# Per-sequence row transfers on the queues of SyncE and ScalarE in a routed three-class MLP with layer norm

## The chip, the cores and the metric

One core of one Trainium2 chip runs the kernel. The metric is the device time of one execution in microseconds (us). Engines are named as in the profile: PE is TensorE, DVE VectorE, ACT ScalarE, POOL GpSimd, SP SyncE; SPq and ACTq are the DMA issues of two of them.

## What is computed

There are 64 sequences of 64 tokens with 256 features. Each sequence has a class from 0 to 2, and only the class's own branch counts:

```python
out_nr  = gelu(x @ w1_nr  + b1_nr)  @ w2_nr  + b2_nr          # class 0
out_tsr = gelu(x @ w1_tsr + b1_tsr) @ w2_tsr + b2_tsr         # class 1
h = gelu(x @ w1_sr + b1_sr)                                   # class 2, 512 wide
out_sr = gelu(h @ w2_sr + b2_sr) @ w3_sr + b3_sr
y = x + where(class == 0, out_nr, where(class == 1, out_tsr, out_sr))
return (y - mean(y)) * rsqrt(var(y) + 1e-5) * gamma + beta
```

The classes are data, known only on the chip. In these inputs they are 23, 26 and 15 sequences.

## The kernel before

**Groups.** The kernel sorts the sequences by class and packs them, 8 at a time, into groups of one class. There are 11 slots for groups (`SLOTS`), at least 8 of them are used (`MIN_GROUPS`), and with these inputs 9 are: 2 of class 2 (called SR, "long"), 4 of class 1 (TSR) and 3 of class 0 (NR), the last 7 being "short". Group g lives in the buffer `xs[g]`, 128 partitions by 4 tokens by 256 features; a sequence is 16 partitions of it, a row 4 KB. With 9 groups there are 72 places and 64 sequences, so 8 places stay empty.

**Table.** DVE and PE compute where each sequence goes (L500 to L541): each sequence's rank within its class, the group in which its class begins (`base`, L523), then `passed`, `nth`, `in_place`, `in_slot` and `row_at` (L521 to L531), a PE product of the last two (L705) and from it the index tables `load_idx` (L538) and `store_idx` (L540). `cls_tab` (L548) holds the class of each group, and every engine loads it into registers and branches on it.

**Rows in and out.** POOL fetches a group with one indirect DMA (`gather`, L299), three of them as soon as `load_idx` is there (`EARLY = 3`) and eight after its weight work (L316). It stores a group with one indirect DMA (`scatter`, L354). SP issues the weights, waits for the first group (L253) before it issues those of the other two classes, and at the end waits for all stores.

**Work of a step.** In step s, PE transposes the rows of group s+1 (L713), makes layer 1 of group s (L732 to L734; `short_first` or `long_first`) and the last layer of group s-1 (`last_layer`, L777 to L788), and for a long group the middle layer (L806 to L808). Each product is three matmuls, since operands are split in a high and a low part. Before its first transposes PE runs ten warm-up matmuls (L814). ACT makes the high parts and the gelus, DVE the low parts, `y` and its moments (L568 to L598; the last of these is `hvar`, which releases POOL). The norm of a group goes over three engines: POOL's power `rstd` (`root`, L331) and `shift` (L335), ACT's z in four tiles (L413), POOL's times gamma (L341) and plus beta (L346) for tiles 0 to 2, DVE's (L603, L605) for tile 3.

**Order on POOL.** `middle(g)` (L359) is root(g), shifted(g), times_gamma(g-1), plus_beta(g-1), scatter(g-1). `final(g)` (L367), for the last group, is times_gamma(g-1) on two tiles, root(g), plus_beta(g-1), scatter(g-1), scatter(g); DVE then takes two tiles of group g-1 (`gamma_beta_two`) and all of group g (L625, L631). `by_place` (L213) chooses between these by the classes of the next groups; PE's `to_f` and `to_x` are the same `last_layer` into `ps_f` or, for the last group, into `ps_x`.

## Time and profile before

| | us |
|---|---|
| median of 3 runs | 112.78 (111.09 to 112.89) |
| the profiled execution | 111.2 |
| its span, first to last instruction | 109.5 |
| PE busy in it | 86.0 |
| POOL busy in it | 68.3 |

The profiled execution took 111.2 us, of which the span is 109.5 us, so 1.7 us lie around the span. The profile gives starts and durations in us from the span's start. "Idle before" and its releaser are inferred from semaphore events; "issue" is time for which the profile shows nothing awaited. Instructions that issue DMAs, load registers or branch are not counted as busy.

### The profile page before, as it was taken

What the parts mean: (1) busy time and instruction counts of PE and PEld (TensorE: products, weight loads), DVE (VectorE), ACT (ScalarE), POOL (GpSimd) and SP (SyncE); (2) the same over time, 40 slices, a digit from 0 to 9 for tenths busy, and PEclk for the clock granted to TensorE, in tenths of its full rate; (3) what the DMA queues carried; (4) which work ended last, traced back from release to release, by engine and by line L of the source; (5) the groups of instructions that cost most, each with busy time, mean ns of one, the idle gap of its engine ahead of it and who ended that gap; (6) DMA issues with size and microseconds to landing.
All of it is one profiled execution on the core that took longest, in us unless ns stands there. A gap on an engine that the chain in (4) does not pass through costs nothing.

```text
span 109.5 us, 1829 instructions
## 1 busy us (share of the span) xinstructions
PE 86.0 (79%) x503; PEld 74.9 (68%) x503; DVE 77.6 (71%) x193; ACT 64.3 (59%) x104; POOL 68.3 (62%) x78
## 2 busy tenths in 40 slices
PE   0269969999999999999999999999999976600000
PEld 0157568868889888798998989989899866500000
DVE  5579084762555572839989899899998889699800
ACT  0575229995986045895977959779595870330000
POOL 6427910019777630000796988979879798999850
PEclk9999999999999999999999999999999999995555
DMA  0794788100498991000000404022040130103153
GB/s 2 264 311 142 234 258 298 34 0 3 94 343 205 419 407 73 0 6 0 0 6 22 175 3 174 6 87 105 6 192 6 73 130 6 54 0 154 40 216 144
DMA packets 5459, 12.84 MB, mean 117 GB/s; under 512 B 688, under 2 KB 2752, under 8 KB 5440
## 3 DMA queue, kind: packets, MB, share of 16 engines
q0 software_dynamic: 2880, 9.96, 25.5%
q1 hardware_dynamic: 2540, 2.63, 7.3%
q8 instruction: 11, 0.18, 0.7%
q14 instruction: 8, 0.07, 0.2%
q10 hardware_dynamic: 20, 0.01, 0.0%
HBM read 8.40 MB, written 4.72 MB: 120 GB/s over the span
## 4 chain that ended last, share of the span: by engine, by line
PE 67%; POOL 13%; DVE 4%; DMA 4%; issue 4%; POOLq 2%; ACT 1%; ACTq 1%
PE ps_a L732 8%; PE ps_a L734 8%; PE ps_a L733 7%; PE ps_x L713 7%; PE ps_f L786 6%; PE ps_f L788 6%; PE ps_f L787 6%; POOL xs L346 4%; POOL xs L341 4%; PE ps_f L814 4%; DMA bias_rows<-L_cond_b_sr_dram 4%; PE ps_f L777 3%; POOL rstd L331 3%; PE ps_b L807 2%; PE ps_b L808 2%
## 5 line engine op out<-in xcount | busy, mean ns | idle before, releaser
L331 POOL TENSOR_TENSOR rstd<-hvar,half 128x4 f32<-128x4 f32 x9 | 9.4, 1040 | 15.6 <-DVE hvar L598 15.5
L788 PE MATMUL ps_f<-wf_hi,f_hi 128*128 x64 | 17.9, 280 | 0.0
L786 PE MATMUL ps_f<-wf_hi,f_lo 128*128 x64 | 17.9, 280 | 0.0
L787 PE MATMUL ps_f<-wf_lo,f_hi 128*128 x64 | 17.9, 280 | 0.0
L732 PE MATMUL ps_a<-x_hi,w_lo 128*128 128x512 f32 x40 | 16.5, 413 | 1.1 <-DVE x_lo L643 1.1
L409 ACT ACTIVATE f_hi<-ps_a,bias_cols 128x512 fp32r<-128x512 f32 x16 | 11.0, 688 | 9.6 <-PE ps_a L808 4.7
L734 PE MATMUL ps_a<-x_hi,w_hi 128*128 128x512 f32 x40 | 15.7, 393 | 0.0
L733 PE MATMUL ps_a<-x_lo,w_hi 128*128 128x512 f32 x40 | 15.6, 390 | 0.0
L299 POOL DMA_INDIRECT xs<-x_dram,load_idx x11 | 11.1, 1012 | 6.5 <-DVE load_idx L538 3.6
L413 ACT ACTIVATE xs<-xs,shift,rstd 128x256 f32<-128x256 f32 x23 | 12.1, 593 | 4.3 <-POOL shift L335 4.3
L346 POOL TENSOR_TENSOR xs<-xs,beta_b 128x768 f32<-128x768 f32 (+1 forms) x8 | 14.1, 1762 | 0.5
L410 ACT ACTIVATE ps_a<-ps_a,bias_cols 128x512 f32<-128x512 f32 x22 | 14.4, 652 | 0.0
L341 POOL TENSOR_TENSOR xs<-xs,gamma_b 128x768 f32<-128x768 f32 (+1 forms) x8 | 14.2, 1779 | 0.0
L564 DVE TENSOR_TENSOR f_lo<-ps_a,f_hi 128x512 fp32r<-128x512 f32 x16 | 10.5, 685 | 3.5 <-ACT ps_a L410 3.1
L568 DVE TENSOR_TENSOR xs<-ps_f,xs 128x1024 f32<-128x1024 f32 x8 | 9.8, 1225 | 4.2 <-PE ps_f L788 4.2
L787 PEld LDWEIGHTS ps_f<-wf_lo,f_hi 128*128 128x128 f32 x64 | 12.0, 188 | 0.7
L786 PEld LDWEIGHTS ps_f<-wf_hi,f_lo 128*128 128x128 f32 x64 | 12.1, 188 | 0.3
L788 PEld LDWEIGHTS ps_f<-wf_hi,f_hi 128*128 128x128 f32 x64 | 12.1, 190 | 0.0
L572 DVE BATCH_NORM_STATS2 stats<-xs 128x6 f32<-128x256 f32 x32 | 11.3, 414 | 0.3
L354 POOL DMA_INDIRECT out_dram<-xs,store_idx x9 | 9.4, 1043 | 3.2 <-POOL xs L346 2.0
L405 ACT ACTIVATE x_hi<-ps_x 128x1024 fp32r<-128x1024 f32 x8 | 8.2, 1027 | 4.0 <-PE ps_x L713 4.0
L313 POOL TENSOR_TENSOR wf_lo<-wf_raw,wf_hi 128x512 fp32r<-128x512 f32 x3 | 4.0, 1337 | 10.2 <-ACT wf_hi L395 10.2
(124 smaller groups left out, 191.3 us busy)
## 6 DMA issues: line engine op xcount, KB each, us to landing
w_raw<-L_cond_w_sr_dram SPq DMA_DIRECT2D x2, 512.0 KB, 4.6
wf_raw<-L_cond_w_sr_dram SPq DMA_DIRECT2D x1, 256.0 KB, 5.3
w_raw<-L_cond_w_tsr_dram SPq DMA_DIRECT2D x1, 256.0 KB, 6.5
w_raw<-L_cond_w_nr_dram SPq DMA_DIRECT2D x1, 256.0 KB, 6.8
wf_raw<-L_cond_w_tsr_dram SPq DMA_DIRECT2D x1, 256.0 KB, 6.9
wf_raw<-L_cond_w_nr_dram SPq DMA_DIRECT2D x1, 256.0 KB, 7.1
xs<-x_dram,load_idx POOLq DMA_INDIRECT x11, 6.5
out_dram<-xs,store_idx POOLq DMA_INDIRECT x9, 3.4
```

Source lines behind the costliest of these rows:

```text
L331: nc.gpsimd.tensor_tensor(rstd[:, g, :], hvar[:, g, :], half[:, :], ALU.pow).then_inc(rstd_step, 1)
L341: nc.gpsimd.tensor_tensor(tiles, tiles, spread(gamma_b, n), ALU.mult).then_inc(gam_pool, 1)
L346: nc.gpsimd.tensor_tensor(tiles, tiles, spread(beta_b, n), ALU.add).then_inc(o_pool, 1)
L410: nc.scalar.activation(bank, bank, ACT.Gelu, bias=bias).then_inc(gelu_done, count)
L413: nc.scalar.activation(dst, xs[g][:, t, :], ACT.Identity, bias=shift[:, g, t:t + 1], scale=rstd[:, g, t:t + 1]).then_inc(z_done, 1)
L572: nc.vector.bn_stats(stats[:, t, :], xs[g][:, t, :]).then_inc(bn_done, 1)
L732: nc.tensor.matmul(dst, w1_lo[:, kt, cols], xh[:, kt, :], start=(kt == 0), stop=False)
L733: nc.tensor.matmul(dst, w1_hi[:, kt, cols], xl[:, kt, :], start=False, stop=False)
L734: mm = nc.tensor.matmul(dst, w1_hi[:, kt, cols], xh[:, kt, :], start=False, stop=(kt == KT - 1))
L786: nc.tensor.matmul(dst, fl[:, kt, toks], w_hi, start=False, stop=False)
L787: nc.tensor.matmul(dst, fh[:, kt, toks], w_lo, start=False, stop=False)
L788: mm = nc.tensor.matmul(dst, fh[:, kt, toks], w_hi, start=False, stop=last)
```

## The change

The index tables go. A table `place_tab` of 2 rows of 88 places holds the number of the sequence at each place and a 1 where there is one. SP and ACT load its entries into registers and issue one plain DMA of 64 KB (16 partitions) for each sequence: SP for all groups but the second half of group 0, which ACT fetches, and the second half of the last group, which ACT stores. All 88 places of the 11 slots are fetched; a store of an empty place is issued with a condition that skips it. `EARLY` is 2: SP issues its half of group 0 and all of group 1, then the weights of the other classes, then the other nine slots, then the stores in order. POOL issues no DMA, runs times gamma ahead of the power, and takes three tiles of the last group but one. `each_step` replaces `by_place`: each step is written out whole for the long class and for the short ones, with the variant for "no further group" (`finish`) ahead of it.

```diff
+        def load_places(eng, regs, row, s, first, n, hi):
+            eng.load(regs[0:n], place_tab[0:1, row, s * PER + first:s * PER + first + n])
+            return [eng.snap(r, min_val=0, max_val=hi) for r in regs[0:n]]
+
+        def x_of(seq):
+            return x[bass.ds(seq, 1), :, :].rearrange("a (q t) h -> (a q) t h", t=TT)
+
+        def out_of(seq):
+            return out[bass.ds(seq, 1), :, :].rearrange("a (q t) h -> (a q) t h", t=TT)
+
+        def rows_of(s, j):
+            return xs[s][j * ROWS:(j + 1) * ROWS, :, :]
+
+        def each_step(eng, cls, step, finish):
+
+
+            for s in range(SLOTS + 1):
+                if s < MIN_GROUPS:
+                    step(s)
+                elif s < SLOTS:
+                    with eng.If(cls[s] > NR):
+                        if s == MIN_GROUPS:
+                            finish(s - 1)
+                        else:
+                            with eng.If(cls[s - 1] < EMPTY):
+                                finish(s - 1)
+                            with eng.Else():
+                                pass
                     with eng.Else():
-                        last(g)
+                        step(s)
                 else:
+                    with eng.If(cls[s - 1] < EMPTY):
+                        finish(s - 1)
+                    with eng.Else():
+                        pass
...
+        def if_next(eng, cls, s, part):
+
+            if s + 1 < MIN_GROUPS:
+                part(s + 1)
+            elif s + 1 < SLOTS:
+                with eng.If(cls[s + 1] < EMPTY):
+                    part(s + 1)
...
-
-            sp.wait_ge(x_loaded[0], 16)
+            seq_regs = [sp.alloc_register(f"sp_seq{j}") for j in range(PER)]
+            taken_regs = [sp.alloc_register(f"sp_taken{j}") for j in range(PER)]
+
+            def fetch(s, n):
+                seqs = load_places(sp, seq_regs, 0, s, 0, n, B - 1)
+                for j in range(n):
+                    sp.dma_start(rows_of(s, j), x_of(seqs[j])).then_inc(x_loaded[s], 16)
+
+
+            sp.wait_ge(place_tab_done, 1)
+            fetch(0, PER // 2)
+            for s in range(1, EARLY):
+                fetch(s, PER)
             for i in (2, 3):
                 sp.dma_start(W_L1[i][0], W_L1[i][1]).then_inc(w_in[i], 16)
             for i in (1, 2):
                 sp.dma_start(W_F[i][0], W_F[i][1]).then_inc(w_in[4 + i], 16)
+            for s in range(EARLY, SLOTS):
+                fetch(s, PER)
             sp.wait_ge(tab_done, 1)
             cls = load_classes(sp, "sp_cls")
-            for s in range(SLOTS):
+
+            def store(g, n):
+                taken = load_places(sp, taken_regs, 1, g, 0, n, 1)
+                seqs = load_places(sp, seq_regs, 0, g, 0, n, B - 1)
+                if n == PER:
+                    sp.wait_ge(o_pool, g + 1)
+                sp.wait_ge(o_dve, 2 * (g + 1))
+                for j in range(n):
+                    sp.dma_start(out_of(seqs[j]), rows_of(g, j), cond=(taken[j] > 0)).then_inc(stored[g], 16)
+
+            def sp_step(s):
+                if s > 0:
+                    store(s - 1, PER)
+            each_step(sp, cls, sp_step, lambda g: store(g, PER // 2))
+            for s in range(MIN_GROUPS - 1):
+                sp.wait_ge(stored[s], 16 * PER)
+            for s in reversed(range(MIN_GROUPS, SLOTS)):
                 with sp.If(cls[s] < EMPTY):
-                    sp.wait_ge(stored[s], 16)
+                    sp.wait_ge(stored[s], 16 * PER)
                 with sp.Else():
                     pass
+            sp.wait_ge(stored[MIN_GROUPS - 1], 16 * PER)
...
-            def gather(s):
-                nc.gpsimd.indirect_dma_start(
-                    out=xs[s][:, :, :].rearrange("p t h -> p (t h)"), out_offset=None, in_=x_rows,
-                    in_offset=bass.IndirectOffsetOnAxis(ap=load_idx[:, s:s + 1], axis=0)
-                ).then_inc(x_loaded[s], 16)
-
-            pool.wait_ge(load_idx_done, 1)
-            for s in range(EARLY):
-                gather(s)
-
...
-            for s in range(EARLY, SLOTS):
-                gather(s)
...
-            def scatter(g, last):
-                if g == 0:
-                    pool.wait_ge(store_idx_done, 1)
-                if not last:
-                    pool.wait_ge(o_pool, g + 1)
-                pool.wait_ge(o_dve, 2 * (g + 1))
-                nc.gpsimd.indirect_dma_start(
-                    out=out_rows, out_offset=bass.IndirectOffsetOnAxis(ap=store_idx[:, g:g + 1], axis=0),
-                    in_=xs[g][:, :, :].rearrange("p t h -> p (t h)"), in_offset=None,
-                    bounds_check=last_row, oob_is_err=False).then_inc(stored[g], 16)
-
+            def pool_group(g):
+                if g > 0:
+                    times_gamma(g - 1, POOL_TT)
                 root(g)
                 shifted(g)
                 if g > 0:
-                    times_gamma(g - 1, POOL_TT)
                     plus_beta(g - 1, POOL_TT)
-                    scatter(g - 1, False)
-
-            def final(g):
-                times_gamma(g - 1, 2)
+
+            def pool_step_of(s):
+                if s > 0:
+                    pool_group(s - 1)
+
+            def pool_finish(g):
+                times_gamma(g - 1, POOL_TT)
                 root(g)
-                plus_beta(g - 1, 2)
-                scatter(g - 1, False)
-                scatter(g, True)
-
-            for g in range(SLOTS):
-                with pool.If(cls[g] < EMPTY):
-                    by_place(pool, cls, g, middle, middle, final)
-                with pool.Else():
-                    pass
+                plus_beta(g - 1, POOL_TT)
+
+            each_step(pool, cls, pool_step_of, pool_finish)
...
+            seq_regs = [act.alloc_register(f"act_seq{j}") for j in range(PER // 2)]
+            taken_regs = [act.alloc_register(f"act_taken{j}") for j in range(PER // 2)]
             w_high(0)
+            act.wait_ge(place_tab_done, 1)
+            for j, seq in enumerate(load_places(act, seq_regs, 0, 0, PER // 2, PER // 2, B - 1)):
+                act.dma_start(rows_of(0, PER // 2 + j), x_of(seq)).then_inc(x_loaded[0], 16)
             w_high(1)
             wf_high(0)
             act.wait_ge(bf_in, 16 * 3)
...
+            def act_finish(g):
+                normed(g - 1)
+                n = PER // 2
+                taken = load_places(act, taken_regs, 1, g, n, n, 1)
+                seqs = load_places(act, seq_regs, 0, g, n, n, B - 1)
+                act.wait_ge(o_dve, 2 * (g + 1))
+                for j in range(n):
+                    act.dma_start(out_of(seqs[j]), rows_of(g, n + j), cond=(taken[j] > 0)).then_inc(stored[g], 16)
+
+            each_step(act, cls, act_step, act_finish)
...
-            dve.wait_ge(dve_step, step[0] - 1)
-            nc.vector.tensor_scalar(passed[:, :], full[:, :], rank[:, 0:1], None, ALU.is_le).then_inc(dve_step, 1)
             dve.wait_ge(dve_step, step[0])
-            nc.vector.tensor_reduce(base[:, :], over_before[:, :, :], AX.XY, ALU.add).then_inc(dve_step, 1)
-            step[0] += 2
-            dve.wait_ge(dve_step, step[0] - 1)
-            chain(nc.vector.tensor_reduce(nth[:, :], passed[:, :], AX.X, ALU.add))
-            chain(nc.vector.scalar_tensor_tensor(out=in_place[:, :], in0=nth[:, :], scalar=-float(PER),
-                                                 in1=rank[:, :], op0=ALU.mult, op1=ALU.add))
-            nc.vector.tensor_scalar(in_slot[:, :], slot_id[:, :], base[:, 0:1], nth[:, 0:1],
-                                    ALU.subtract, ALU.is_equal).then_inc(place_done, 1)
-            nc.vector.scalar_tensor_tensor(out=row_at[:, :], in0=row_place[:, :], scalar=in_place[:, 0:1],
-                                           in1=row_val[:, :], op0=ALU.is_equal, op1=ALU.mult
-                                           ).then_inc(place_done, 1)
+            chain(nc.vector.tensor_reduce(base[:, :], over_before[:, :, :], AX.XY, ALU.add))
+            chain(nc.vector.scalar_tensor_tensor(out=place[:, :], in0=base[:, :], scalar=float(PER), in1=rank[:, :],
+                                                 op0=ALU.mult, op1=ALU.add))
+            nc.vector.tensor_scalar(at_place[:, :], place_id[:, :], place[:, 0:1], None, ALU.is_equal
+                                    ).then_inc(at_place_done, 1)
 
             chain(nc.vector.tensor_reduce(groups[:, :], over[0:1, :, :], AX.X, ALU.add))
             chain(nc.vector.tensor_tensor_scan(ends[:, :], groups[:, :], zeros[:, :], 0.0, ALU.add, ALU.add))
-            dve.wait_ge(rows_ps, 1)
-            nc.vector.tensor_scalar(load_idx[:, :], rows_pt, float(NROWS), float(NROWS - 1), ALU.add, ALU.min
-                                    ).then_inc(load_idx_done, 1)
-            nc.vector.tensor_scalar(store_idx[:, :], rows_pt, float(NROWS), None, ALU.add
-                                    ).then_inc(store_idx_done, 1)
+            dve.wait_ge(places_ps, 1)
+            nc.vector.tensor_copy(place_tab[:, :, :], places_pt).then_inc(place_tab_done, 1)
             for r in range(ROUTES):
                 nc.vector.tensor_scalar(ended[:, :, r], slot_id[0:1, :], ends[:, r:r + 1], None, ALU.is_ge
...
-                dve.wait_ge(z_done, TT * g + (1 if n == 1 else TT))
-                nc.vector.tensor_tensor(tiles, tiles, spread(gamma_b, n), ALU.mult).then_inc(gam_dve, 1)
+            def gamma_beta_one(g):
+                dve.wait_ge(z_done, TT * g + 1)
+                nc.vector.tensor_tensor(ps_z[:, 0, 0:H], ps_z[:, 0, 0:H], gamma_b[:, :], ALU.mult).then_inc(gam_dve, 1)
                 dve.wait_ge(gam_dve, g + 1)
-                nc.vector.tensor_tensor(out_tiles, tiles, spread(beta_b, n), ALU.add).then_inc(o_dve, 2)
-
-            def gamma_beta_one(g):
-                gamma_beta(g, ps_z[:, :, 0:H], xs[g][:, TT - 1:TT, :], 1)
-
-            def gamma_beta_two(g):
-                gamma_beta(g, ps_a[0][:, 0, :].rearrange("p (t h) -> p t h", t=2), xs[g][:, 2:TT, :], 2)
+                nc.vector.tensor_tensor(xs[g][:, TT - 1, :], ps_z[:, 0, 0:H], beta_b[:, :], ALU.add
+                                        ).then_inc(o_dve, 2)
...
-            pe.wait_ge(place_done, 2)
-            nc.tensor.matmul(rows_pt, row_at[:, :], in_slot[:, :], start=True, stop=True).then_inc(rows_ps, 1)
+            pe.wait_ge(at_place_done, 1)
+            nc.tensor.matmul(places_pt[:, 0, :], seq_ones[:, 0:1], at_place[:, :], start=True, stop=True)
+            nc.tensor.matmul(places_pt[:, 1, :], seq_ones[:, 1:2], at_place[:, :], start=True, stop=True
+                             ).then_inc(places_ps, 1)
...
-                pe.wait_ge(x_loaded[g], 16)
+                pe.wait_ge(x_loaded[g], 16 * PER)
...
+            def pe_step(s):
                 if s > 0:
-                    with pe.If(cls[s - 1] < EMPTY):
-                        by_place(pe, cls, s - 1, to_f, to_f, to_x)
+                    pe.wait_ge(x_lo_done, upto_x(s))
+                    if_next(pe, cls, s, transpose_x)
+                with pe.If(cls[s] < TSR):
+                    long_first(s)
+                    if s > 0:
+                        last_layer(s - 1, ps_f)
+                    long_second(s)
+                with pe.Else():
+                    with pe.If(cls[s] < NR):
+                        short_first(TSR, s)
                     with pe.Else():
-                        pass
-                if s < SLOTS:
-                    with pe.If(cls[s] < TSR):
-                        long_second(s)
+                        short_first(NR, s)
+                    if s > 0:
+                        last_layer(s - 1, ps_f)
+
+            each_step(pe, cls, pe_step, lambda g: last_layer(g, ps_x))
```

The same recasting into `act_step`, `dve_step_of` and `pool_step_of` keeps the order of ACT's and DVE's instructions within a step; DVE takes one tile of the last group but one where it took two, and POOL three where it took two.

On POOL, the end of the program as it runs with 9 groups; before, the group before the last and the last. The names are those of the lines above, with `xs7` the last group but one.

```order
L331 TENSOR_TENSOR rstd<-hvar,half 128x4
L335 TENSOR_TENSOR shift<-rstd,neg_mean 128x4
L341 TENSOR_TENSOR xs6<-xs6,gamma_b 128x768
L346 TENSOR_TENSOR xs6<-xs6,beta_b 128x768
L354 DMA out_dram<-xs6,store_idx 1024x1024
...
L341 TENSOR_TENSOR xs7<-xs7,gamma_b 128x512
L331 TENSOR_TENSOR rstd<-hvar,half 128x4
L346 TENSOR_TENSOR xs7<-xs7,beta_b 128x512
L354 DMA out_dram<-xs7,store_idx 1024x1024
L354 DMA out_dram<-xs8,store_idx 1024x1024
```

And now:

```order
L370 TENSOR_TENSOR xs6<-xs6,gamma_b 128x768
L360 TENSOR_TENSOR rstd<-hvar,half 128x4
L364 TENSOR_TENSOR shift<-rstd,neg_mean 128x4
L375 TENSOR_TENSOR xs6<-xs6,beta_b 128x768
...
L370 TENSOR_TENSOR xs7<-xs7,gamma_b 128x768
L360 TENSOR_TENSOR rstd<-hvar,half 128x4
L375 TENSOR_TENSOR xs7<-xs7,beta_b 128x768
```

Gamma stands ahead of the power, the three DMAs are gone, and the last two products have 768 columns for 512.

On SP, the store of the last group, as it runs with 9 groups; before, SP's rows there are only branches and waits. An ISA row computes an address from a register, TENSOR_LOAD fills the registers (once for the sequence numbers, once for the ones that say a place is taken).

```order
L209 TENSOR_LOAD place_tab
L210 ISA
L209 TENSOR_LOAD place_tab
L210 ISA
L296 ISA
L296 DMA out_dram<-xs8 16x1024
L296 ISA
L296 DMA out_dram<-xs8 16x1024
L296 ISA
L296 DMA out_dram<-xs8 16x1024
L296 ISA
L296 DMA out_dram<-xs8 16x1024
```

The store of any other group has eight such DMAs on SP, and in the fetch there is one address row for each DMA too.

## Rows read from the trace of the kernel before

**Rows 1.** The page, part 4: the chain that ended last, by engine.

```profile
PE 67%; POOL 13%; DVE 4%; DMA 4%; issue 4%; POOLq 2%; ACT 1%; ACTq 1%
```

**Rows 2.** Busy time by stretch, with TensorE clock, DMA share and GB/s.

```profile
core 0: us, PE busy (x) PEld busy (x) DVE busy (x) ACT busy (x) POOL busy (x), PEclk, DMA share, GB/s
42.20:83.40 41.20, 41.20 (x276) 37.54 (x275) 35.06 (x84) 33.83 (x56) 26.91 (x24) 1.00 0.14 53
105.00:106.00 1.00, 0.00 (x0) 0.00 (x0) 0.00 (x0) 0.00 (x0) 0.83 (x1) 0.50 0.89 360
```

**Rows 3.** Timeline of the start: start us, us, instruction [idle before <-releaser].

```profile
5.29 0.17 DVE L523 TENSOR_REDUCE base<-over_before 64x1 f32<-64x32 f32 x1
...
5.99 0.34 DVE L531 SCALAR_TENSOR_TENSOR row_at<-row_place,in_place,row_val 64x128 f32<-64x128 f32 x1
...
7.09 0.17 DVE L538 TENSOR_SCALAR load_idx<-ps_b 128x11 int32<-128x11 f32 x1 [0.49 <-PE ps_b L705]
7.13 1.06 ACT L391 ACTIVATE w_hi<-w_raw 128x1024 fp32r<-128x1024 f32 x1 [0.45 <-DMA w_raw<-L_cond_w_sr_dram]
...
7.35 4.64 PE L814 MATMUL ps_f<-warm_x,ones 128*128 128x512 f32 x10
...
11.91 1.30 PEld L713 LDWEIGHTS ps_x<-ident,xs 128*128 128x128 f32 x8 [0.65 <-DMA xs<-x_dram,load_idx]
...
14.48 0.19 PEld L732 LDWEIGHTS ps_a<-x_hi,w_lo 128*128 128x128 f32 x1 [1.27 <-issue]
...
15.97 1.03 PE L713 MATMUL ps_x<-ident,xs 128*128 128x128 f32 x8
```

**Rows 4.** DMA issues: the timeline of SPq, and the page, part 6 (us to landing).

```profile
4.32 0.24 SPq L247 DMA_DIRECT2D bf_raw<-L_cond_b_tsr_dram  x1
4.61 0.25 SPq L247 DMA_DIRECT2D bf_raw<-L_cond_b_nr_dram  x1
4.90 0.36 SPq L250 DMA_DIRECT2D gamma_b<-L_cond_gamma_dram  x1
...
cond_col<-itok_B_dram SPq DMA_DIRECT2D x1, 0.2 KB, 2.3
out_dram<-xs,store_idx POOLq DMA_INDIRECT x9, 3.4
```

**Rows 5.** Timeline of POOL at the end.

```profile
93.39 1.05 POOL L331 TENSOR_TENSOR rstd<-hvar,half 128x4 f32<-128x4 f32 x1
...
94.67 1.81 POOL L341 TENSOR_TENSOR xs<-xs,gamma_b 128x768 f32<-128x768 f32 x1
...
99.72 1.28 POOL L341 TENSOR_TENSOR xs<-xs,gamma_b 128x512 f32<-128x512 f32 x1
...
101.97 1.26 POOL L346 TENSOR_TENSOR xs<-xs,beta_b 128x512 f32<-128x512 f32 x1
103.51 1.05 POOL L354 DMA_INDIRECT out_dram<-xs,store_idx  x1 [0.29 <-POOL xs L346]
104.87 0.96 POOL L354 DMA_INDIRECT out_dram<-xs,store_idx  x1 [0.30 <-issue]
```

**Rows 6.** Timeline of DVE and ACT at the end.

```profile
92.83 0.16 DVE L598 SCALAR_TENSOR_TENSOR hvar<-m,diff 128x4 f32<-128x4 f32 x1
...
93.71 0.42 DVE L605 TENSOR_TENSOR xs<-ps_z,beta_b 128x256 f32<-128x256 f32 x1
...
94.96 0.70 DVE L579 TENSOR_TENSOR ps_x<-ps_x,xs 128x512 f32<-128x512 f32 x1 [0.83 <-PE ps_x L788]
95.75 1.04 ACT L413 ACTIVATE ps_a<-xs,shift,rstd 128x256 f32<-128x256 f32 x2
...
98.64 0.19 DVE L598 SCALAR_TENSOR_TENSOR hvar<-m,diff 128x4 f32<-128x4 f32 x1
...
102.02 1.66 DVE L631 SCALAR_TENSOR_TENSOR xs<-ps_x,rstd,beta_b 128x256 f32<-128x256 f32 x4
```

**Rows 7.** Timeline of PE where the last group's last layer begins.

```profile
91.19 0.49 PE L777 MATMUL ps_x<-bf_parts,ones 128*128 x1 [1.54 <-issue]
```

More of the change, by code:

```diff
@@ L80, in build_cond_mlp @@
         rank = sb("rank", [B, 1])
-        full = sb("full", [B, PER])
-        passed = sb("passed", [B, PER])
-        nth = sb("nth", [B, 1])
-        in_place = sb("in_place", [B, 1])
         slot_id = sb("slot_id", [B, SLOTS])
-        in_slot = sb("in_slot", [B, SLOTS])
-        row_place = sb("row_place", [B, P])
-        row_val = sb("row_val", [B, P])
-        row_at = sb("row_at", [B, P])
-        load_idx = sb("load_idx", [P, SLOTS], I32)
-        store_idx = sb("store_idx", [P, SLOTS], I32)
+        place_id = sb("place_id", [B, PLACES])
+        seq_ones = sb("seq_ones", [B, 2])
+        place = sb("place", [B, 1])
+        at_place = sb("at_place", [B, PLACES])
+        place_tab = sb("place_tab", [1, 2, PLACES], I32)
         groups = sb("groups", [1, ROUTES])
```

226 lines of the change are left out of this document (73 added, 153 removed).

## The prediction

> **What bounds the kernel now.** I read first the chain that ended last, then busy time by stretch, then the timelines of the two ends. The chain gives PE 67% and POOL 13% [rows 1]. The stretches say where each rules: from 42.2 to 83.4 us PE is busy for all of the 41.2 us, while POOL is busy for 26.91 [rows 2]. There, taking POOL's DMA work away or giving SP more to do is worth nothing, provided rows arrive in time. So the change can act at two places: the start, and the end behind PE, where POOL's ordered list (power, gamma, beta, store) and then the last stores set the end.
>
> At the start ten warm-up matmuls run from 7.35 to 11.99, and the first transposes follow at once; the rows of group 0 were there at 11.91, when PE's loads stopped waiting for that DMA [rows 3]. Two things end together: earlier rows alone gain nothing. At the end POOL's last product ends at 101.97 + 1.26 = 103.23, the last scatter is issued at 104.87 [rows 5], lands about 3.4 us later [rows 4] at 108.3, and some 1.2 us on the span ends at 109.5.
>
> **The table chain.** Before, it went from `base` (5.29) over `in_place` and `row_at` (5.99 + 0.34) and PE to `load_idx`, done at 7.26 [rows 3]. Now it is `base`, `place`, `at_place`, PE, one copy: three instructions fewer ahead of PE, about 0.5 us, so the table stands at 6.8. POOL's two memsets of weight parts move up beside this chain and may give part of that back.
>
> **The fetches.** SP must load registers. The trace shows no such load alone; after its first transposes PE loads 11 registers in an idle stretch of at most 1.27 us [rows 3], so 0.5 us for four is my estimate, and 0 to 1.3 the bound. Then comes the cost on which everything hangs: the interval between two plain 64 KB DMAs on one queue, with an address row for each. Call it d. From below: two tiny DMAs on SP start 0.29 us apart [rows 4]. From above: POOL's two last indirect issues start 1.36 us apart [rows 5]. One over 128 partitions occupied SP for 0.36 us [rows 4]. Sixteen partitions lie between the tiny and the wide one, and the address row adds something; I take d = 0.37. For the landing after an issue, the tiniest took 2.3 and a scatter 3.4 us [rows 4]; I take 2.6.
>
> SP's four and ACT's four of group 0 start at 7.3 to 8.4 and land at 11.0, 0.9 us before the warm-ups end. SP's eight of group 1 begin after another load at 9.4, the last at 12.0, landing at 14.6; PE transposes them at 15.97 [rows 3], a margin of 1.4 us. The four issues on ACT stand ahead of its weight copy that began at 7.13 [rows 3] and push that and two small copies back by 2 us; ACT's next job is the high part of x after the transposes that start at 11.91, so this is covered with about 1.5 us to spare. The later weights go out at about 12.4 instead of when group 0 landed, near 11.9: half a microsecond on loads that are read ten microseconds later. The other 72 fetches take 72 x 0.37 = 27 us of SP beside PE's work; each group has a step of nearly 7 us, so it pays until d is above 0.8. Start: 0.
>
> **POOL at the end.** PE no longer idles 1.54 us before the last layer of the last group [rows 7], if that idle time came from the long way in the code to it: `finish` now follows at once. DVE waited 0.83 us for PE there [rows 6], so its sums start when its previous product ends, 93.71 + 0.42 = 94.1, and the last `hvar`, done at 98.83, is done at 98.0. POOL waited for no one at 93.39 but its own scatter; `hvar` of group 7 was ready at 92.99 [rows 6]. So power and shift end at 93.0 + 1.35 = 94.35. ACT's four z took to 96.79 from 94.7 [rows 5, 6], so now until 96.45. Then POOL: gamma on three tiles 1.81 [rows 5] to 98.3, power 1.05 to 99.35, beta on three tiles, 1.8 by the same row, to 101.15. Before this end was 103.23: 2.1 us earlier. Split: two scatters between groups out, the third tile (some 0.5 us for each product) in. Gamma ahead of the power hides gamma in the wait for `hvar`; its price is that the last power starts 0.3 us after its `hvar`. DVE's four last products (1.66 us, [rows 6]) are ready at about 102.5, before SP reaches them.
>
> **The stores at the end.** Here the change pays back. Group 7 is eight DMAs on SP, ready at 101.15, and four of group 8 follow on the same queue; ACT's other four run beside them. SP's last starts 11 intervals on: 101.25 + 11 x 0.37 = 105.3. Landing 2.6, then the same 1.2 us: 109.1. The stores thus start 2.1 us sooner, their issue takes 4.0 us where two scatters needed 1.6 from 103.23, and the landing is 0.8 shorter. The waits that SP now walks at its end lie under that landing.
>
> **Sum.** 109.1 against 109.5: -0.4 us. The profiled execution would be 110.8 for 111.2; that execution lies 1.6 us under the median of the runs, 112.78, and on that scale I say 112.4. The forecast's own range: d = 0.29 and landing 2.3 give 101.25 + 3.2 + 2.3 + 1.2 = 107.9, d = 0.45 and landing 3.4 give 110.8, so 111.2 to 114.1. About 2% (2.3 us) is what a measurement of this kernel can tell from no change.
>
> **Rival 1, narrow transfers (slower).** Each DMA now covers 16 of 128 partitions. If such a transfer cannot use the whole width, its rate falls. The whole width moved 360 GB/s in the stores' stretch [rows 2]; one part in eight of the partitions could be held to anything between an eighth and all of that. At a quarter, 90 GB/s, 64 KB take 0.73 us, and both queues share it. End: 15 real stores, 101.25 + 14 x 0.73 + 2.6 + 1.2 = 115.3. Start: group 0 lands at 7.3 + 7 x 0.73 + 2.6 = 15.0, 3.0 us late, and group 1 adds up to 2. Together 9 to 11 us. If transfers overlap in part, an effective 0.5 us gives 112 at the end and half a microsecond at the start: 112.8, or 116 on the scale of the median. I price this rival at 117. It decides from an interval of 0.42, where the end is what it was. For it: nothing in the profile shows narrow large transfers keeping their rate. Against it: successive sequences touch different partitions and could overlap. The middle would hide it either way.
> The Trainium skill speaks against the change here: "SBUF — State Buffer", section "Door 1: The DMA port swizzle", says that bandwidth follows the SBUF ports reached and gives 104 GB/s for partitions 0 to 15; 64 KB would take 0.63 us. By it, as an estimate, the end is at 113.9 and the start 3 us late. No row here shows it.
>
> **Rival 2, PE's way through the code.** The long and short variants are now written out whole, so at step 8 PE skips more. In the instruction lists, before, PE skipped 104 rows between the last layer of step 7 and the first product of step 8 without a gap, and 183 rows before the 1.54 us of [rows 7]. Now it skips about 131 at step 8 and none at step 9. If 131 is already too many, the idle time moves to 83.4, where DVE and POOL follow PE closely, and group 7's `hvar` and all behind it come 1.4 us later: 110.5, or 113.8 on the scale of the median.
> The Trainium skill, "Runtime: NRT & Kernel Launch", section "Instruction fetch mechanics", says that a taken branch to a target outside the two pages held stalls for a fetch. The gap in the trace agrees with such a rule, but does not show its cause.
>
> **Rival 3, faster.** If the issue is as cheap as the tiny DMAs', landing is 2.0 and the closing time shrinks with POOL's queue empty, the span is 107.2: 110.3 on the scale of the median. For it: POOL's end improves by 2.1 in any case. Against it: twelve issues in a row on one queue.
>
> **How the numbers follow.** Forecast 45%, rival 1 30%, rival 2 10%, rival 3 15%. Beyond 2% faster: rival 3 and a little of the forecast's edge, 0.18. Slower: rival 1 less its mild part, and the edge of the forecast with rival 2's, 0.33. The rest, 0.49, is within 2%. The range runs from rival 3 to just above the priced rival 1: 110.2 to 118.5.
>
> **What would show it.** In the new trace: DMA issues on SP at intervals near 0.37 (0.6 and more: rival 1, or a dear issue); transposes of group 0 at 11.9 and of group 1 near 16.0 without a wait for the DMA; POOL's last product ending near 101.2; no PE gap at 83.4 and none before the last layer; SP's last store starting near 105.3. The forecast is wrong if the landing of group 7's stores grows with each of them, or if PE waits for rows at any step.

## The result, and the profile after

The changed kernel takes 130.44 us (median of 4 runs, 130.06 to 130.92) where the kernel before takes 112.03 (111.09 to 112.89): a ratio of 1.173, interval 1.168 to 1.179. Two of the four executions of the kernel before (112.78 and 112.89) fell in a slower state of the chip, so the ratio is against the other two, 111.09 and 111.28, and the 1.6 us that the forecast added for "the scale of the median" come from that state. The forecast was 112.4, with a range up to 118.5. It was wrong, far outside the range.

The profiled execution took 130.06 us, its span is 128.2 us (before 109.5). The page of the changed kernel, its parts 1 to 4 in extract (PEclk is the granted TensorE clock in tenths):

```profile
PE 89.4 (70%) x505; PEld 76.7 (60%) x505; DVE 77.7 (61%) x189; ACT 64.5 (50%) x104; POOL 48.5 (38%) x58
...
PE   0296399999999999999999999999996000000000
...
PEclk9999855999999999999999999999999755555555
DMA  1958485342343432533314525262443422562633
...
q1 hardware_dynamic: 7180, 12.14, 40.7%
...
PE 61%; DVE 12%; DMA 5%; issue 2%; ACTq 2%; ACT 1%; DVEq 1%
```

No engine is busier than before by more than 0.2 us, apart from PE's 3 us, and POOL has lost the 20 us that were to go. Yet in the last nine slices of 40, some 28 us, PE does nothing, while the DMA engines go on, two to six tenths busy. The chain of waits [as rows 1] ends in products of DVE at 108.3 and shows little of what follows, since DMA issues are no busy time. What follows is in the timeline of SP's queue (start us, us from the start of the first issue to the end of the last, instruction, count), the answer to [rows 4]:

```profile
8.24 6.83 SPq L273 DMA_DIRECT2D xs<-x_dram  x12
...
18.04 46.07 SPq L273 DMA_DIRECT2D xs<-x_dram  x72
67.31 58.72 SPq L296 DMA_DIRECT2D out_dram<-xs  x68
```

These last two rows are the whole result. SP fetches until 64.1, reads its tables for 3.2 us, and then stores without a pause until 126.0; 2.2 us later the span ends. Group 0 was ready at 60.49, when POOL's last product on it ended; its stores begin at 67.3, 6.8 us late. From group to group the stores are 7.06 us apart on average (5.6 to 8.8), while groups come every 6.99 and the last two sooner, so the backlog never goes away: group 7 is ready at 107.04 and its first store starts at 117.6. Computation ended long before; timelines of POOL and DVE, the answer to [rows 5, 6]:

```profile
58.63 1.86 POOL L375 TENSOR_TENSOR xs<-xs,beta_b 128x768 f32<-128x768 f32 x1
...
102.07 1.68 DVE L589 TENSOR_TENSOR diff<-stats 128x4 f32<-128x4 f32 x1
...
106.65 1.65 DVE L627 SCALAR_TENSOR_TENSOR xs<-ps_x,rstd,beta_b 128x256 f32<-128x256 f32 x4
...
104.25 1.02 POOL L360 TENSOR_TENSOR rstd<-hvar,half 128x4 f32<-128x4 f32 x1 [0.52 <-DVE hvar L599]
105.24 1.80 POOL L375 TENSOR_TENSOR xs<-xs,beta_b 128x768 f32<-128x768 f32 x1
```

The first row is POOL's last product on group 0. POOL is done at 107.04, DVE at 108.3. The start is worse too; the timeline of PE, ACT's queue and SP's, the answer to [rows 3]:

```profile
8.20 2.00 ACTq L445 DMA_DIRECT2D xs<-x_dram  x4
...
13.88 1.10 PE L698 MATMUL ps_x<-ident,xs 128*128 128x128 f32 x8 [2.05 <-DMA xs<-x_dram]
...
16.18 0.77 PE L713 MATMUL ps_a<-x_hi,w_lo 128*128 128x512 f32 x1 [1.21 <-DVE x_lo L639]
```

PE waits 2.05 us for the first rows, 13.88 instead of 11.91. With that idle time behind it its granted clock falls from 2.4 to 1.2 GHz (the two 5s in PEclk): products follow each other at 0.43 us instead of 0.23 from 16.2 to 22.4. The next steps are 4.8 us late: the transposes of step 2 start at 46.80 for 42.01.

What one issue costs is in the instructions of the fetch's line, the store's line and the register load's, on SP (count: duration in ns, least/median/most):

```profile
L273 SPq MOVE xs<-x_dram x84: 29/29/38, 8.2 to 63.7; - x84
L273 SPq DMA_DIRECT2D xs<-x_dram x84: 315/316/1407, 8.2 to 63.8; - x84
L273 SPq FUSED_REGOPS  x73: 37/37/43, 8.6 to 63.7; - x73
...
L296 SPq FUSED_REGOPS  x68: 174/174/200, 67.0 to 125.4; - x68
L296 SPq DMA_DIRECT2D out_dram<-xs x68: 73/315/1170, 67.3 to 125.7; - x68
...
L209 SPq TENSOR_LOAD <-place_tab x29: 298/524/545, 7.4 to 123.1; - x29
```

A fetch mostly starts 0.50 us after the one before, a store 0.63, since the register step (FUSED_REGOPS) takes 174 ns with the condition and 37 without. A store that its condition skips still takes 0.40. A group of eight adds its register loads: across one load two fetches start 1.26 us apart, and between the last store of a group and the first of the next lie 2.2, with two loads. Now and then an issue takes up to 1.4 us; the trace shows no cause. With all this a group of fetches takes 5.12 us on average (46.07 / 9) and one of stores 7.06.

### The profile page after: what moved, and what is told of

It is laid out like the page before. It is cut to its first block, busy times and chain, and to the rows that moved or that the text cites. A ratio compares the mean times of both kernels' runs of the same rounds, so it can differ in the third digit from the quotient of the medians.

```text
span 128.2 us, 2202 instructions
## 1 busy us (share of the span) xinstructions
PE 89.4 (70%) x505; PEld 76.7 (60%) x505; DVE 77.7 (61%) x189; ACT 64.5 (50%) x104; POOL 48.5 (38%) x58
## 4 chain that ended last, share of the span: by engine, by line
PE 61%; DVE 12%; DMA 5%; issue 2%; ACTq 2%; ACT 1%; DVEq 1%
PE ps_a L713 8%; PE ps_a L714 8%; PE ps_a L715 8%; PE ps_x L698 7%; PE ps_f L766 6%; PE ps_f L767 6%; PE ps_f L765 6%; DMA xs<-x_dram 3%; PE ps_f L756 3%; DMA cond_col<-itok_B_dram 2%; PE ps_b L780 1%; PE ps_b L779 1%; PE ps_b L781 1%; DVE diff L589 1%; DVE ps_x L621 1%
## 5 line engine op out<-in xcount | busy, mean ns | idle before, releaser
L370 POOL TENSOR_TENSOR xs<-xs,gamma_b 128x768 f32<-128x768 f32 x8 | 14.7, 1838 | 12.0 <-ACT xs L429 12.0
L713 PE MATMUL ps_a<-x_hi,w_lo 128*128 128x512 f32 x40 | 17.7, 443 | 1.2 <-DVE x_lo L639 1.2
L714 PE MATMUL ps_a<-x_lo,w_hi 128*128 128x512 f32 x40 | 16.5, 414 | 0.0
L715 PE MATMUL ps_a<-x_hi,w_hi 128*128 128x512 f32 x40 | 16.5, 412 | 0.0
L375 POOL TENSOR_TENSOR xs<-xs,beta_b 128x768 f32<-128x768 f32 x8 | 14.8, 1846 | 0.0
L429 ACT ACTIVATE xs<-xs,shift,rstd 128x256 f32<-128x256 f32 x24 | 12.6, 592 | 0.0
L698 PE MATMUL ps_x<-ident,xs 128*128 128x128 f32 x72 | 10.3, 290 | 2.0 <-DMA xs<-x_dram 2.0
L698 PEld LDWEIGHTS ps_x<-ident,xs 128*128 128x128 f32 x72 | 8.9, 150 | 3.3 <-DMA xs<-x_dram 2.8
```

Of the source, the lines that this page charges most:

```text
L370: nc.gpsimd.tensor_tensor(tiles, tiles, spread(gamma_b, n), ALU.mult).then_inc(gam_pool, 1)
L375: nc.gpsimd.tensor_tensor(tiles, tiles, spread(beta_b, n), ALU.add).then_inc(o_pool, 1)
L429: nc.scalar.activation(dst, xs[g][:, t, :], ACT.Identity, bias=shift[:, g, t:t + 1], scale=rstd[:, g, t:t + 1]).then_inc(z_done, 1)
L698: mm = nc.tensor.transpose(ps_x[:, kt, t * P:(t + 1) * P], xs[g][:, t, kt * P:(kt + 1) * P], ident[:, :])
L713: nc.tensor.matmul(dst, w1_lo[:, kt, cols], xh[:, kt, :], start=(kt == 0), stop=False)
L714: nc.tensor.matmul(dst, w1_hi[:, kt, cols], xl[:, kt, :], start=False, stop=False)
```

## The experiments

e1, e2, e3, e4, e7, e8 and e10 are one execution each. The spans of the changed kernel's four executions go from 128.2 to 129.2 us, so a difference of 1 us in them says nothing.

**e1, fewer fetches.** Two of the eleven slots hold nothing for this input; the change fetches rows for them all the same. Here SP skips them.

```diff
-            for s in range(EARLY, SLOTS):
+            for s in range(EARLY, MIN_GROUPS):
                 fetch(s, PER)
...
+            for s in range(MIN_GROUPS, SLOTS):
+                with sp.If(cls[s] < EMPTY):
+                    fetch(s, PER)
```

> SP does not fetch the two slots that stay empty (16 of 88 fetches). Theory A (SP's stream of issues is the bound: about 5.1 us per slot fetched, 7.1 us per group stored, back to back from 67.3 us): the stores begin when group 0 is ready, near 60.6, not 67.3, and the span falls by those 6.7 us to 121.5; the other 3.5 us of the saving turn into waiting for group 0. Theory B (narrow transfers move their bytes slowly): about the same fall, so this run tells A and B from a third, that the end is set by compute: then nothing changes, 128.

Measured: 120.42 us, span 118.6, 2.9 us below the expectation. With sixteen issues fewer on SP the span is 9.6 us shorter. SP's rows:

```profile
18.16 37.38 SPq L273 DMA_DIRECT2D xs<-x_dram  x56
59.05 57.24 SPq L301 DMA_DIRECT2D out_dram<-xs  x68
```

The stores start 8.3 us sooner, and the end follows. Not all of it is the edit's. SP is free at 55.5 and now waits for group 0, which is ready at 58.71: the fetches held the stores up by the 6.8 us of the changed kernel. Group 0 is ready 1.8 us sooner here, as PE's lower clock lasted 3.4 us and not 6.8 in this execution, and the stores took 1.5 us less. So the rows that nobody reads cost about 7 us, over a third of the loss.

**e2, the same count, fewer bytes.** The sixteen fetches stay, with 8 KB each instead of 64.

```diff
+                    if s < 9:
                         sp.dma_start(rows_of(s, j), x_of(seqs[j])).then_inc(x_loaded[s], 16)
+                    else:
+                        sp.dma_start(rows_of(s, j)[:, 0:1, 0:128], x_of(seqs[j])[:, 0:1, 0:128]).then_inc(x_loaded[s], 16)
```

> The 16 fetches of the empty slots are still issued, but carry 8 KB each, not 64 KB. Theory A (cost per issued DMA): SP's interval stays 0.50 us, the first store still starts near 67.3, span 128. Theory B (cost per byte in a transfer of 16 partitions): SP gets through these 16 some 6 us sooner, first store near 61, span 121.5.

Measured: 128.79 us, span 127.0.

```profile
17.98 35.85 SPq L274 DMA_DIRECT2D xs<-x_dram  x56
54.77 8.95 SPq L276 DMA_DIRECT2D xs<-x_dram  x16
66.93 57.85 SPq L299 DMA_DIRECT2D out_dram<-xs  x68
```

With an eighth of the bytes the sixteen still take 8.95 us of SP (9.34 in the changed kernel), and the stores start at 66.93 for 67.31. The span is 1.2 us shorter, hardly more than two executions differ. From 64 KB down to 8 KB the price is by the DMA, not by the byte.

**e3, e4, e5: one side at a time.** Three kernels keep the change's layout of the code and its order on POOL (gamma ahead of the power) and give back POOL's indirect DMAs for the stores (e3), for the fetches (e4) and for both (e5). The long table chain is back too; e3 and e4 make both tables, which starts PE 0.5 us later (first transposes at 14.40 for 13.88, and 12.52 for e5's 12.00). The core of the edits, as POOL has it again:

```diff
+            def gather(s):
+                nc.gpsimd.indirect_dma_start(
+                    out=xs[s][:, :, :].rearrange("p t h -> p (t h)"), out_offset=None, in_=x_rows,
+                    in_offset=bass.IndirectOffsetOnAxis(ap=load_idx[:, s:s + 1], axis=0)
+                ).then_inc(x_loaded[s], 16)
...
-            def store(g, n):
...
+                    scatter(g - 1, False)
```

> Fetches stay one plain DMA per sequence on SP, stores go back to one indirect DMA per group on POOL (with the old index tables beside the new one). Theory A with a late start: rows of group 0 come 2 us late and the TensorE clock falls once, 4.7 us as in the changed kernel, plus about 0.3 for the longer table chain; the end is POOL's: span 113 to 114. If the stores' backlog is not the main cost: above 120.

> Fetches go back to indirect DMAs on POOL, stores stay per sequence on SP. Theory A: no late start (transposes at 12.0, full clock); SP stores from about 56 us at 7.1 us per group, a little slower than groups get ready, so it is 3 to 4 us behind at the last two, and then eight and four more issues: span 116 to 118. If the rows' late start mattered more than the stores: below 113.

> Everything of the change but its DMAs: fetches and stores are indirect on POOL as before, with gamma ahead of the power, three tiles on POOL for the last group but one, and the steps written out. If the DMAs per sequence are the whole loss: span 108.3 to 109.5 and a ratio of 0.98 to 1.00 to the kernel before. If the new code layout costs PE time at its jumps: a gap on PE near 83 us and 110 or more.

Measured, as spans, so that the rows can be compared: before 109.5; e5 112.0; e3 116.2; e4 117.0; the change 128.2. From e5, fetches by SP cost 4.2 us, stores by SP 5.0, both 16.2: 7.0 us more than the two together. That surplus is the shared queue, where the stores of group 0 wait 6.8 us for the fetches. In e4, with SP free for stores, its rows read

```profile
57.38 57.45 SPq L301 DMA_DIRECT2D out_dram<-xs  x68
```

It begins as soon as group 0 is ready and keeps pace with PE (6.8 us a group, where groups come every 6.96), but after POOL's last product at 103.39 it still has twelve stores and two sets of register loads to issue: the last starts at 114.5. The times are 118.03 us (e3, span 2.2 above its expectation, which left out what e5 loses) and 118.7 (e4, as expected). e5 has four executions: 113.68 us, ratio 1.021 (1.017 to 1.025), span 2.5 above before. The expectation was a gain, and it missed; e6 and e9 look for the cause.

**e6, gamma ahead of the power alone.** The kernel before with this one edit:

```diff
+                if g > 0:
+                    times_gamma(g - 1, POOL_TT)
                 root(g)
                 shifted(g)
                 if g > 0:
-                    times_gamma(g - 1, POOL_TT)
```

> The kernel before with one change: on POOL, times gamma of the group before runs ahead of the power and shift. Theory: POOL's list at the end shortens, since gamma of groups 5 and 6 runs in POOL's waits for DVE: span 107.6, 1.9 less, ratio 0.983. Rival: root is held up by ACT's z and nothing is gained: 109.5.

Measured: 112.24 us, ratio 1.009 (1.0065 to 1.0116). A small loss, clear of its interval, instead of a gain. DVE and POOL in e6:

```profile
92.81 1.11 DVE L589 TENSOR_TENSOR diff<-stats 128x4 f32<-128x4 f32 x1
...
92.03 1.85 POOL L341 TENSOR_TENSOR xs<-xs,gamma_b 128x768 f32<-128x768 f32 x1
```

`diff` is an operation on 128x4 that takes 0.17 us elsewhere. Here it ends at 93.92, when POOL's gamma ends, 93.88. The last `diff` takes 0.93 in the same way, behind gamma at 98.87. So gamma, meant to fill POOL's wait for `hvar`, holds up the very chain on DVE that makes `hvar`: group 7's is ready at 94.34 where it was 92.99. The Trainium skill, "SBUF — State Buffer", section "SBUF: two separate sides", says that VectorE and GpSimd share a port pair that one of them can lock; the rows agree with that rule.

**e7, a warm start.** Fifteen warm-up matmuls instead of ten, so that PE is idle for less time ahead of the rows.

> The changed kernel with 15 warm-up matmuls, not 10, so that PE works until about 13.8 us, when the rows of group 0 land. Theory (the idle 2 us let the granted clock fall to half from 16 to 22 us, which costs 2.9 us): the clock stays full, the end of compute moves from 108.3 to 105.4. The span stays near 128, because SP's issues set it. Rival (the clock falls whatever PE does ahead): compute ends at 108.3 or later.

Measured: 131.62 us, span 129.9. PE is idle for 1.39 us instead of 2.05, the clock stays at its full level, and steps come 2.85 us sooner (43.95 for 46.80). The end does not: SP's stores start at 68.09 and take 59.56. The lower clock costs 2.9 us of computation and, in this kernel, nothing of the time. The span is even 1.7 us longer, by longer pauses between SP's issues, whose cause is not known.

**e8, no registers for the fetch.** Sequence numbers fixed when the kernel is built; no register load, no address step. The kernel leaves out the sorting by class at the fetch, so sequences pass through another class's branch; the work is the same.

```diff
-                seqs = load_places(sp, seq_regs, 0, s, 0, n, B - 1)
                 for j in range(n):
-                    sp.dma_start(rows_of(s, j), x_of(seqs[j])).then_inc(x_loaded[s], 16)
+                    sp.dma_start(rows_of(s, j), x_of((s * PER + j) % B)).then_inc(x_loaded[s], 16)
```

> SP's fetches take their sequence number from the place number at build time: no register load and no address row in a fetch (so the rows of the sequences are mixed up). Theory: the interval of two fetches falls from 0.50 to about 0.36 us, a slot from 5.1 to about 3.5 us, the stores begin near 60 when group 0 is ready, span 121.5. If the interval stays at 0.50, the DMA itself and not the address work sets it.

Measured: 123.27 us, span 121.4, as expected, though the interval of two fetches fell to 0.46 and not to 0.36. The 72 fetches take 37.35 us instead of 46.07 and end at 52.4; the stores start at 61.03, as soon as group 0 is ready (60.7). But the first transposes come later still, at 14.56. The fetch's instructions from 16 to 24 us, and after them part 2 of the page, 3 us to a slice:

```profile
L272 SPq DMA_DIRECT2D xs<-x_dram x18: 419/420/429, 16.0 to 23.9; - x18
...
DMA to landing us min/median/max: 5.0/5.1/5.2
```

```profile
DMA  2879999999995444430036261644426231266533
GB/s 22 316 221 178 131 271 222 149 144 144 151 161 127 132 112 119 104 92 0 0 65 108 38 100 35 103 76 80 85 49 103 51 54 23 50 108 105 95 65 68
```

These fetches land 5.1 us after their issue; in the changed kernel it is 2.1 (median of all). From 21 to 36 us the DMA engines are taken up by nine tenths or more and move 144 to 161 GB/s. The stores of before moved 360 at 0.89 [rows 2]. Transfers of 16 neighbouring partitions are thus held to some 150 GB/s here, 0.44 us for 64 KB: just under the issue interval. The queue shows the same: the landing grows from 2.1 to 4.8 us over SP's first eight fetches, which share the DMA engines with ACT's four, then falls by some 0.01 us from one fetch to the next, and is back at 2.2 from 38 us on. There the DMA engines are busy for 0.46 of the time, and the interval is 0.46 us still: the issue sets it, and not the transfer.

**e9, the layout of the code alone.** e5 with POOL's order as before: what is left is PE's, DVE's and ACT's new code and the third tile for POOL in group 7.

```diff
-                if g > 0:
-                    times_gamma(g - 1, POOL_TT)
                 root(g)
                 shifted(g)
                 if g > 0:
+                    times_gamma(g - 1, POOL_TT)
```

> All of the change but its DMAs (rows fetched and stored by GpSimd's indirect DMAs as before), and now with GpSimd's order as before too: power, shift, gamma, beta, store. What is left is the new layout of the code (long and short variants written out whole) and the third tile for GpSimd in the last group but one. Theory (the cost of e5 is two costs: about 0.9 us for gamma ahead of the power, as in e6, and 1.4 us for the layout, namely one gap of 0.9 us on TensorE at the first short step and 0.07 us more on each short step): span 110.8 to 111.3, ratio to before 1.008 to 1.016, the gap still there. Rival (the whole excess of e5 is GpSimd's products blocking VectorE): span 109.3 to 110.0, ratio 0.998 to 1.004, whatever the gap.

Measured: 114.13 us, ratio 1.026 (1.024 to 1.028), span 112.7. Both theories fall: taking gamma's early place away made it slower, not faster. The timelines of PE and POOL say where 3.2 us of span come from:

```profile
41.64 1.03 PE L716 MATMUL ps_x<-ident,xs 128*128 128x128 f32 x8
43.94 0.47 PE L731 MATMUL ps_a<-x_hi,w_lo 128*128 128x512 f32 x1 [1.27 <-DVE f_lo L585]
50.09 1.04 PE L716 MATMUL ps_x<-ident,xs 128*128 128x128 f32 x8
...
94.89 1.05 POOL L365 TENSOR_TENSOR rstd<-hvar,half 128x4 f32<-128x4 f32 x1
...
101.22 1.82 POOL L375 TENSOR_TENSOR xs<-xs,gamma_b 128x768 f32<-128x768 f32 x1
```

Step 2, the first of the short ones, takes 8.45 us instead of 6.97, with a gap on PE after its transposes, where PE branches past the code of the long class; the same gap is in e5 (0.88) and e4 (1.01). The row names DVE's `f_lo` as its releaser, but in e5 the gap has none. Group 7's power starts 1.50 later than in [rows 5]. The third tile makes gamma 1.82 for 1.28 and beta 1.80 for 1.26: 1.1 together. The last 0.6 lies behind the last store's issue. So with three tiles POOL's list is the bound at the end, and gamma ahead of the power seems to give back 0.5% there (e5's 1.021 against e9's 1.026; the intervals overlap a little, so this is not shown); with two it costs 0.9% (e6). The gap itself needs the new layout and POOL's fetches together: the changed kernel, e1, e3 and e7, with the same layout and SP's fetches, show no gap there (step 7.0). Its cause was not found.

**e10, the same DMAs on partitions spread out.** Sequence j of a group on every eighth partition instead of on 16 neighbours.

```diff
-            return xs[s][j * ROWS:(j + 1) * ROWS, :, :]
+            return xs[s][j:P:PER, :, :]
```

> The changed kernel, but sequence j of a group lies on the partitions j, j + 8, j + 16 ... instead of on 16 neighbours; same DMAs, same bytes, same registers. Theory (the end is bound by SP's issue, 72 fetches and 68 stores one after another): fetch interval 0.50 and store interval 0.63 us as before, span 127.5 to 129. Rival 1 of the prediction (a transfer of 16 neighbouring partitions is held to a part of the width): the landing after the issue falls from 2.0 us, ACT's four land sooner than 3.3 us after the issue, the first transposes start at 13.2 or before instead of 13.9, and if the intervals were the transfers' they fall too, span 122 to 125.

Measured: 152.91 us, span 151.1, far from both. Two effects of opposite sign. The fetch's instructions, PE's start, ACT's landing and SP's queue:

```profile
L273 SPq DMA_DIRECT2D xs<-x_dram x84: 495/496/1505, 8.2 to 78.4; - x84
...
12.96 1.10 PE L698 MATMUL ps_x<-ident,xs 128*128 128x128 f32 x8 [1.67 <-DMA xs<-x_dram]
...
xs<-x_dram ACTq DMA_DIRECT2D x4, 64.0 KB, 2.3
...
20.22 58.71 SPq L273 DMA_DIRECT2D xs<-x_dram  x72
82.16 66.78 SPq L296 DMA_DIRECT2D out_dram<-xs  x68
```

The rows land sooner: ACT's four after 2.3 us instead of 3.3, and the first transposes start at 12.96 instead of 13.88 although the issue is slower. So the 16 neighbours do hold the transfer back where two queues issue at once. But the issuing instruction itself takes 0.496 us instead of 0.316, and the intervals are 0.68 for a fetch and 0.82 for a store. That is 0.18 for each of 140 DMAs, 25 us, and 23 of them come out at the end: SP's last issue ends at 148.9 instead of 126.0. Bytes, rows and registers are the same, so what a plain DMA costs its queue depends on how its 16 partitions lie. PE's clock stayed at 2.4 GHz through the start of this run, though PE was idle for 1.67 us before its first transposes and for 1.85 before its first products.

**e11, a version between the two.** The kernel before, with its fetches and tables. SP stores groups 5 and 6 by sequence from a place table made late, and in the last group the power comes ahead of gamma.

```diff
+            for g in range(SP_FROM, SLOTS - 2):
+                if g + 2 < MIN_GROUPS:
+                    store(g)
...
-                    scatter(g - 1, False)
+                    if g - 1 < SP_FROM:
+                        scatter(g - 1, False)
...
-                times_gamma(g - 1, 2)
                 root(g)
+                times_gamma(g - 1, 2)
```

> The kernel before, with its indirect fetches and its table chain, but (a) SP stores groups 5 and 6 by one plain DMA for each sequence from a place table worked out late, so that GpSimd's two indirect stores at 92.31 and 98.64 us (1.05 us each and 0.29 us of waiting ahead) are gone; (b) the last two groups are still stored by GpSimd; (c) in the last group the power comes ahead of gamma. Theory (GpSimd's list at the end is the bound, per-sequence stores on an idle SP are hidden): power of group 7 at 93.0 instead of 93.39, power of group 8 at 98.9 instead of after gamma, last product ends at 102.4 instead of 103.23, span 108.4 to 109.0, ratio 0.985 to 0.997. Rival (16 stores on SP collide with something: the final waits, the transfers of the last groups; or the VectorE waits for GpSimd's products all the same): span 109.5 or above.

Measured, eight executions: 110.88 us against 111.24 of before on this chip, ratio 0.9967 (0.9956 to 0.9978), span 109.1, at the weak edge of the expectation.

```profile
92.77 10.75 SPq L289 DMA_DIRECT2D out_dram<-xs  x16
...
98.95 1.02 POOL L388 TENSOR_TENSOR rstd<-hvar,half 128x4 f32<-128x4 f32 x1 [0.55 <-DVE hvar L659]
...
102.84 1.05 POOL L411 DMA_INDIRECT out_dram<-xs,store_idx  x1 [0.29 <-POOL xs L403]
```

It is 0.3% faster than the kernel before, which is little, but its interval leaves out 1, and 15% faster than the changed one. POOL's scatter of group 7 starts 0.67 us sooner than in [rows 5], and 0.4 of that is left at the end of the span; the gap of [rows 7] is still there (1.71), so the last `hvar` is no sooner than before. Per-sequence stores on an idle SP can be hidden. Which of the two edits gives the 0.3% was not separated.

## Why the prediction was wrong

**The step that failed** is in the part on the fetches: "The other 72 fetches take 72 x 0.37 = 27 us of SP beside PE's work; each group has a step of nearly 7 us, so it pays until d is above 0.8." It compares the fetches of a group with a step. But SP is one ordered list: all fetches stand ahead of all stores, and each group needs both. The sum to make was: start 18.0, nine groups of fetches at 5.12, tables 3.2, stores 58.7, landing and end 2.2, which is 128.2. That is the span. By the forecast SP had to be ready for group 7's stores near 101; it was ready for group 0's at 67.3, where they had waited since 60.5, and for group 7's at 117.6. The stores run no faster than groups come, so the 7 us never go away.

**The term that was mis-sized** is what a DMA costs SP. d was 0.37, bounded by 0.29 and 0.45; it measured 0.50 for a fetch and 0.63 for a store. The issuing instruction, 0.316 us, does lie between the tiny and the wide one [rows 4]; the interval does not, because the register work around it adds to it. The prediction named the address row, gave it next to nothing, and left out the condition. The register loads were given 0.5 us once for each part of the start and never again; they take 0.8 us of each group of fetches (1.26 for 0.50) and 1.6 of each of stores (2.2 for 0.63), and the long issues some 0.4 of each. The wrong step and the wrong size belong together. With d = 0.37 and free loads the serial sum is 18 + 27 + 68 x 0.37 = 70, and the step does no harm; with 0.50 and 0.63 and still no loads, 18 + 36 + 43 = 97, just below 101. Only with the loads, the tables and the long issues does it pass. e8, which frees the fetches of loads and address steps, shows the 7 us (span 121.4).

**The fetches of empty slots** were counted among the 72 and priced at nothing. e1 shows them at about 7 us of the span.

**The start, "0",** was wrong by 2 us, plus the clock. The table was there at 7.4, not 6.8, and after the register load the issues began at 8.2, not 7.3. The landing was 3.3 for ACT's four, not 2.6, while two queues of narrow transfers ran at once; with the rows spread out it was 2.3 (e10). I had kept the clock out of the start altogether; e7 puts it at 2.9 us of computation. None of it sets the end of the changed kernel. In e3, where SP has only fetches, it is the 4.2 us: its transposes of group 4 come at 53.90 for 49.75 in e5; 0.5 of that is the longer table chain.

**POOL's end** was forecast at 101.15 and came at 107.04. Of these 5.9 us, 4.8 are the late start and 0.5 are short steps of 6.99 us for 6.89. `diff`, 1.68 us for 0.17, held by gamma, adds 1.5, and 0.9 came back elsewhere. I had called gamma hidden, at a price of 0.3 us; e6 shows a loss of 0.9% by itself. The row that gave it away was in the trace of before, beside POOL's beta, and I did not ask why it was three times its usual length:

```profile
97.89 0.48 DVE L588 TENSOR_TENSOR diff<-stats 128x4 f32<-128x4 f32 x1
```

**The end**, 11 intervals from 101.25, was forecast at 105.3. Even in e4, without backlog, the last store starts at 114.5, 11 us after POOL's last product: a store of group 6 still in the queue, two rounds of loads, and intervals of 0.63.

**Rival 1** was priced at 117 and given 30%. Its mechanism is real: near 150 GB/s for narrow transfers (e8), a loss at the start that spreading makes smaller, 12.96 for 13.88 (e10). The Trainium skill's port rule, "SBUF — State Buffer", section "Door 1: The DMA port swizzle", points the right way; its 104 GB/s is for one transfer over 16 partitions, and e8's 150 are several at once on neighbouring ranges, so no run tests that figure. But the mechanism doesn't set the end: at 0.44 us a transfer is quicker than its issue. The time went by another way than the forecast and all rivals. The interval from which rival 1 was to decide, 0.42, does not follow from its own sum: with its 14 intervals the end is what it was at 0.32, with the forecast's 11 at 0.40. At 0.63 us a transfer the start would be 2.3 us late and not 3 (7.3 + 7 x 0.63 + 2.6 = 14.3), and rival 3's 107.2 would be 110.5 on the scale of the median, not 110.3. **Rival 2** foresaw a gap at step 8; there is none in the changed kernel, nor the 1.54 us of [rows 7] before the last layer, as forecast. With POOL's fetches a gap appears all the same, at step 2 (e4, e5, e9). **Rival 3** fell with d.

## What to carry to other kernels

Before work moves to an idle queue, write that queue's whole list as one serial sum, register loads, conditions and useless transfers included, and compare when its last item can start with when its data is ready: a step that fits by itself says nothing. One indirect DMA that costs POOL 1.0 us replaces eight plain ones that cost SP 5 to 7, so the exchange can pay only for the few groups where SP is idle, and there it gave at most 0.3% (e11). And work put into a wait must not take a port from the engine that ends that wait.

## What the runs showed of the hardware

- A plain 64 KB DMA with its address in a register occupies SP for 0.50 us, with a condition 0.63, skipped by its condition 0.40; on partitions eight apart 0.18 more. With the address fixed when the kernel is built it is 0.46 (e8), though its issuing instruction takes 0.42 for 0.316. Eight times fewer bytes change it little (8.95 us for 9.34 for sixteen, register loads included).
- A load of eight registers from SBUF takes SP 0.52 us, one of four 0.30, and the pause between two groups of stores, with two such loads, 2.2.
- Transfers to 16 neighbouring partitions moved about 150 GB/s with the DMA engines nine tenths busy, and their landing grew from 2.1 to 4.8 us while SP issued one every 0.46 us beside ACT's four; alone at that interval it was 2.2 (e8).
- A 128x4 operation on DVE took up to 1.68 us in the changed kernel (2.59 for `m` in e5) while POOL multiplied 128x768, and ended with it.
- PE's idle 2 us before its first transposes were followed by 6.8 us at 1.2 GHz, worth 2.9 us (e7). It does not follow from the length of the gap alone: after 1.65 us in e1 came 3.4 us at 1.2 GHz, after 1.67 in e10 none.
